# A DTW-aligned cross-attention and routed experts block on one core: context loaded as two halves, its other layout queued later, last squares' steps reordered

## What is computed

```python
def align_one(small, large):              # small: context (154 x 512), large: layernorm(x) (2048 x 512)
    D = pairwise_euclidean(small, large)  # 154 x 2048 distances
    R = dtw_cost(D)                       # R[i,j] = D[i,j] + min(R[i-1,j], R[i,j-1], R[i-1,j-1])
    i_idx, j_idx, valid = backtrack(R, T_small, T_large)
    contrib = small[i_idx] * valid[:, None]
    return zeros((T_large, d)).at[j_idx].add(contrib)

x = x + tanh(g_xattn[0]) * vmap(align_one)(ctx_1024, layernorm(x))
x = x + tanh(g_ffn[0]) * ffn(layernorm(x), gate_w, expert_w)   # top 2 of 8 experts, softmax weights
```

## Time and profile before

| | us |
|---|---|
| median of 3 runs | 623.06 |
| lowest and highest | 621.59, 623.34 |
| the profiled execution | 623.45 |
| its span, first to last instruction | 621.6 |
| TensorE busy in it | 468.9 |
| VectorE busy | 286.5 |
| ScalarE busy | 241.4 |
| GpSimd busy | 237.3 |

### The profile page before, as it was taken

One profiled execution on the slowest core, in us unless ns is written; L12 is line 12 of the kernel. 1 busy time (PEld: TensorE's weight loads), 2 busy tenths in 40 slices (PEclk: granted clock), 3 DMA queues, 4 the chain that ended last, 5 costly groups with the idle time before them and its releaser, 6 DMA issues.

```text
span 621.6 us, 7820 instructions
## 1 busy us (share of the span) xinstructions
PE 468.9 (75%) x2118; PEld 276.3 (44%) x2118; DVE 286.5 (46%) x1522; ACT 241.4 (39%) x449; POOL 237.3 (38%) x228
## 2 busy tenths in 40 slices
PE   5999667567100001828999999999999999999994
PEld 5999644344100001315445544444444444444441
DVE  4878989999988885999861400000000000000000
ACT  4477685444400000484779322222222333333331
POOL 5900230000000000004432456676567667666853
PEclk9899877977555555776999999999999999999998
DMA  8962269710051004376878957787787778678875
GB/s 253 391 221 74 70 153 251 188 27 1 0 202 69 1 1 141 124 283 214 272 191 245 283 98 134 136 160 135 120 162 133 134 141 153 113 140 153 147 125 67
DMA packets 56108, 91.78 MB, mean 148 GB/s; under 512 B 19263, under 2 KB 19263, under 8 KB 55907
## 3 DMA queue, kind: packets, MB, share of 16 engines
q0 software_dynamic: 18016, 43.00, 37.5%
q1 hardware_dynamic: 33523, 39.88, 19.5%
q10 hardware_dynamic: 4528, 8.41, 4.2%
HBM read 50.05 MB, written 41.21 MB: 147 GB/s over the span
## 4 chain that ended last, share of the span: by engine, by line
PE 59%; DVE 31%; DMA 4%; issue 4%; ACT 1%; POOL 0%; SPq 0%; POOLq 0%; ACTq 0%; DVEq 0%
PE psum L1694 40%; DVE met L923 5%; PE psum L1679 5%; PE psum L1472 5%; DVE waves L836 5%; DVE tokens L926 3%; DVE tokens L861 3%; DVE shf L827 2%; PE psum L1459 2%; DVE tokens L839 2%; DVE tokens L985 2%; PE psum L1621 2%; DVE tokens L830 2%; DMA ar<-in_ctx_dram 1%; DVE waves L826 1%
## 5 line engine op out<-in xcount | busy, mean ns | idle before, releaser
L1694 PE MATMUL psum<-big,tokens 128*128 x624 | 280.6, 593 | 0.3 <-ACT tokens L1393 0.3
L1694 PEld LDWEIGHTS psum<-big,tokens 128*128 128x128 f32 x624 | 112.5, 190 | 112.9 <-issue 112.9
L637 POOL DMA_INDIRECT tokens<-x_rows,gather_ids x78 | 79.1, 1014 | 45.7 <-issue 21.3
L650 POOL DMA_INDIRECT out_dram<-work,add_ids x40 | 63.2, 1580 | 53.6 <-DMA out_dram<-work,add_ids 26.3
L650 POOL DMA_INDIRECT out_dram<-prow,add_ids x38 | 59.9, 1577 | 45.9 <-DMA out_dram<-prow,add_ids 11.9
L657 POOL DMA_DIRECT2D out_dram<-tokens x2 | 1.8, 912 | 172.3 <-DVE tokens L985 172.3
L1403 ACT ACTIVATE work<-psum,tile_shares 128x512 f32<-128x512 f32 x40 | 27.5, 686 | 99.4 <-PE psum L1694 93.5
L1403 ACT ACTIVATE prow<-psum,tile_shares 128x512 f32<-128x512 f32 x38 | 26.1, 686 | 92.1 <-PE psum L1694 92.1
L1364 ACT ACTIVATE stage<-tokens,nm 128x512 f32<-128x512 f32 x32 | 21.7, 713 | 96.8 <-DVE tokens L985 96.7
L1679 PEld LDWEIGHTS psum<-ident,tokens 128*128 128x128 f32 x312 | 39.0, 143 | 39.0 <-issue 33.7
L1590 PE MATMUL psum<-side,work 128*128 128x2 f32 x8 | 1.9, 356 | 70.9 <-DVE work L944 70.9
(11 more groups left out here) (320 smaller groups left out, 614.2 us busy)
## 6 DMA issues: line engine op xcount, KB each, us to landing
tokens<-in_x_dram SPq DMA_DIRECT2D x16, 1024.0 KB, 11.1
stage<-in_L_ffn_expert_w_dram ACTq DMA_DIRECT2D x8, 1024.0 KB, 6.2
x_rows<-stage SPq DMA_DIRECT2D x32, 256.0 KB, 2.5
out_dram<-tokens SPq DMA_DIRECT2D x6, 1024.0 KB, 8.1
tokens<-dist_rows SPq DMA_DIRECT2D x52, 64.0 KB, 2.2
dist_rows<-work SPq DMA_DIRECT2D x16, 160.0 KB, 2.0
out_dram<-tokens POOLq DMA_DIRECT2D x2, 1024.0 KB, 5.1
dist_rows<-prow SPq DMA_DIRECT2D x5, 256.0 KB, 10.4
```

What stands on the lines that cost most here:

```text
L637: pool.indirect_dma_start(out=xin[:, n % UX, :], out_offset=None, in_=x2_d[b][:, :], in_offset=bass.IndirectOffsetOnAxis(ap=gids[:, b, j:j ...
L650: pool.indirect_dma_start(out=out_d.rearrange("b t c -> (b t) c"), in_=yout(n), in_offset=None, out_offset=bass.IndirectOffsetOnAxis(ap=ai ...
L1694: ins = nc.tensor.matmul(psum[:, UP + n % UP, :], xinT[:, n % UX, c, :], expT[:, bass.ds(own, 1), c, :].rearrange("p o d -> p (o d)"), sta ...
```

## The change

The context is loaded a second time in another layout, two halves of 77 rows on 77 partitions each (`ctxh`, in the second half of `stage`), and these loads stand first on SP's queue. `ctx_centred`, `context` and `context_turned` work on the halves. The 128 + 26 layout (`am`, `ar`) is still loaded, but behind four groups of x, and only GpSimd's splitting uses it; GpSimd now waits for its loads instead of for VectorE. One constant matrix (`turn_h`) takes the place of two, and one product that of two in `context_norms`. The context's means for the gate come from `cmean`, by one more product for each of four sums in TensorE's `ctx_gate`; two ScalarE instructions of `ctx_gate_rows` go. At the end of the front, the roots of the last group stand ahead of the distances of units 10 and 11, unit 14's max is done by ScalarE and unit 15's by VectorE, and the last squares stand after wave steps 0 and 1 and after step 2, where they stood after steps 0 to 2 and after steps 3 and 4.

```diff
...
@@ -167,7 +167,9 @@
         aa = sb("ctx_norms", [P, 2, B])
-        aam, aar = aa[:, 0, :], aa[0:SR, 1, :]
+        aam = aa[:, 0, :]
+        spare = prow[:, B * T:2 * B * T].bitcast(F32)[:, 2 * GT * SG:]
+        cmean = spare[:, 0:2 * B * G].rearrange("p (h b e) -> p h b e", h=2, b=B)
         auxs = sb("aux", [P, NT])
@@ -177,7 +179,8 @@
         stage = stagef[:, :].rearrange("p (h k c) -> p h k c", h=2, k=GT)
-        ctxc = stage[:, 0, :, :]
+        ctxc = stage[0:H, 0, :, :]
+        ctxh = stage[0:H, 1, :, :]
         sq = prow[:, B * T:2 * B * T].bitcast(F32)[:, 0:2 * GT * SG].rearrange("p (r k n) -> p r k n", r=2, k=GT)
...
@@ -426,14 +430,17 @@
         def _(sp):
+            for h in range(2):
+                sp.dma_start(ctxh[:, 2 * h:2 * h + 2, :], ctx_d[:, h * H:(h + 1) * H, :].rearrange("b p c -> p b c")).then_inc(
+                    s_ch, 16)
+            for g in ORDER[:4]:
+                sp.dma_start(x[:, GT * g:GT * g + GT, :], x_v[g]).then_inc(s_x[g], 16)
             sp.dma_start(am[:, :, :], ctx_d[:, 0:SM, :].rearrange("b p c -> p b c")).then_inc(s_ctx, 16)
-            for g in ORDER[:1]:
-                sp.dma_start(x[:, GT * g:GT * g + GT, :], x_v[g]).then_inc(s_x[g], 16)
             sp.wait_ge(s_zero, 1)
             for k in range(3):
                 sp.dma_start(ar[32 * k:32 * k + SR, :, :],
                              ctx_d[:, SM:S, :].rearrange("b p c -> p b c")).then_inc(s_ctr, 16)
-            for g in ORDER[1:]:
+            for g in ORDER[4:]:
                 sp.dma_start(x[:, GT * g:GT * g + GT, :], x_v[g]).then_inc(s_x[g], 16)
...
@@ -555,9 +560,10 @@
                            allow_small_or_imprecise_dtypes=True).then_inc(s_late, 1)
-            nc.gpsimd.memset(gwT[:, :, E], 1.0 / C).then_inc(s_late, 1)
-
-            pool.wait_ge(s_cc, 2)
+            nc.gpsimd.memset(gwT[:, :, E], 0.0).then_inc(s_late, 1)
+
+            pool.wait_ge(s_ctx, 16)
+            pool.wait_ge(s_ctr, 48)
             n = 0
...
@@ -703,21 +709,17 @@
 
-            def ctx_centred(r):
-                a = am if r == 0 else ar[0:SR3, :, :]
-                n = P if r == 0 else SR3
-                if r == 0:
-                    v.wait_ge(s_ctx, 16)
-                else:
-                    v.wait_ge(s_ctr, 48)
+            def ctx_centred(h):
+                v.wait_ge(s_ch, 32)
                 for b in range(B):
-                    ins = v.bn_stats(cst[0:n, r, b, :], a[:, b, :])
+                    ins = v.bn_stats(cst[0:H, h, b, :], ctxh[:, 2 * h + b, :])
                 link(ins)
                 for b in range(B):
-                    ins = v.bn_aggr(cmv[0:n, r, b, :], cst[0:n, r, b, :])
+                    ins = v.bn_aggr(cmv[0:H, h, b, :], cst[0:H, h, b, :])
                 link(ins)
                 for b in range(B):
-                    ins = v.tensor_scalar(ctxc[0:n, 2 * r + b, :], a[:, b, :], cmv[0:n, r, b, 0:1], None, ALU.subtract)
+                    ins = v.tensor_scalar(ctxc[:, 2 * h + b, :], ctxh[:, 2 * h + b, :], cmv[0:H, h, b, 0:1], None,
+                                          ALU.subtract)
                 ins.then_inc(s_cc, 1)
@@ -725,6 +727,7 @@
                 v.tensor_scalar(aa[:, :, :], aa[:, :, :], float(C), float(C), ALU.mult, ALU.add).then_inc(s_aam, 1)
+                v.tensor_scalar(cmean[:, :, :, E], cmv[:, :, :, 0], -2.0, None, ALU.mult).then_inc(s_aam, 1)
 
@@ -761,15 +764,15 @@
             def last_squares_by_row():
-                for u in (NU - 2, NU - 1):
-                    b, h, g = UNITS[u]
-                    v.wait_ge(s_d2, u + 1)
-                    v.wait_ge(s_dd, u - 1)
-                    if h:
-                        v.wait_ge(s_aab, 2)
-                    v.tensor_scalar(dsq[0:HP, u % 2, :], psum[0:HP, u % 2, :], (aab if h else aam)[0:HP, b:b + 1], 0.0,
-                                    ALU.add, ALU.max).then_inc(s_dv, 1)
-
+                u = NU - 1
+                b = UNITS[u][0]
+                v.wait_ge(s_d2, u + 1)
+                v.wait_ge(s_dd, u - 1)
+                v.wait_ge(s_aab, 2)
+                v.tensor_scalar(dsq[0:HP, u % 2, :], psum[0:HP, u % 2, :], aab[0:HP, b:b + 1], 0.0,
+                                ALU.add, ALU.max).then_inc(s_dv, 1)
+
+            v.memset(cmean[:, :, :, :], 0.0)
             link(v.memset(cmv[:, :, :, :], 0.0))
@@ -839,14 +842,13 @@
 
-            for s in range(0, 3):
+            for s in range(0, 2):
                 step(s)
             squares_by_token(NG - 1, (0, 1))
-            for s in range(3, 5):
-                step(s)
+            step(2)
             squares_by_token(NG - 1, (2, 3))
             last_squares_by_row()
-            for s in range(5, NS):
+            for s in range(3, NS):
                 step(s)
@@ -1186,14 +1188,11 @@
             def context_turned(n):
-                b, r = n % B, n // B
+                b, h = n % B, n // B
                 act.wait_ge(s_aTp, n + 1)
-                lo, cnt = (0, SM) if r == 0 else (SM, SR)
-                got = psum[:, AT[n], 0:CH * cnt].rearrange("p (c i) -> p c i", c=CH)
-                if r == 0:
-                    nc.scalar.mul(aT[:, b, :, 0:H], got[:, :, 0:H], -2.0)
-                nc.scalar.mul(aT[:, b, :, S + H - lo - cnt:S + H - max(lo, H)][:, :, ::-1],
-                              got[:, :, max(lo, H) - lo:cnt], -2.0).then_inc(s_aT, 1)
+                got = psum[:, AT[n], 0:CH * H].rearrange("p (c i) -> p c i", c=CH)
+                rows = aT[:, b, :, h * H:(h + 1) * H]
+                nc.scalar.mul(rows[:, :, ::-1] if h else rows, got, -2.0).then_inc(s_aT, 1)
 
@@ -1220,17 +1219,17 @@
                 b, h, g = UNITS[u]
-                if u < NU - 2:
+                if u < NU - 1:
                     act.wait_ge(s_d2, u + 1)
...
                         act.wait_ge(s_dd, u - 1)
-                    nc.scalar.activation(dsq[0:HP, u % 2, :], psum[0:HP, 6 + u % 2, :], ACT.Relu,
+                    nc.scalar.activation(dsq[0:HP, u % 2, :], psum[0:HP, u % 2 if u == NU - 2 else 6 + u % 2, :], ACT.Relu,
                                          bias=(aab if h else aam)[0:HP, b:b + 1]).then_inc(s_dq, 1)
                     act.wait_ge(s_dq, u + 1)
                 else:
-                    act.wait_ge(s_dv, u + 3 - NU)
+                    act.wait_ge(s_dv, 1)
                 if u >= 2:
@@ -1255,13 +1254,14 @@
                 roots(i - 1)
+                if i == NG - 1:
+                    roots(i)
                 if i == 2:
...
                     distances(2 * (i - 2) + h)
-            roots(NG - 1)
             def codes_laid(k):
@@ -1293,10 +1293,8 @@
                 for to, n, at in ((cgx, P, 320), (cgr, SR3, 352)):
-                    nc.scalar.mul(to[:, :, 0:E], psum[0:n, 3, at:at + B * G].rearrange("p (b e) -> p b e", e=G)[:, :, 0:E],
+                    nc.scalar.mul(to[:, :, :].rearrange("p b e -> p (b e)"), psum[0:n, 3, at:at + B * G],
                                   -0.5).then_inc(s_cgc, 1)
-                for r, (to, n) in enumerate(((cgx, P), (cgr, SR3))):
-                    nc.scalar.mul(to[:, :, E], cmv[0:n, r, :, 0], tgates[0:n, 0:1]).then_inc(s_cgc, 1)
 
@@ -1424,22 +1422,19 @@
             def context(n):
-                b, r = n % B, n // B
-                pe.wait_ge(s_cc, r + 1)
+                pe.wait_ge(s_cc, n // B + 1)
                 if n == B:
                     pe.wait_ge(s_gwc, B + 1)
-                cnt = SM if r == 0 else SR
                 for c in range(CH):
-                    ins = nc.tensor.transpose(psum[:, AT[n], c * cnt:(c + 1) * cnt], ctxc[0:cnt, n, c * P:(c + 1) * P],
-                                              ident[0:cnt, 0:cnt])
+                    ins = nc.tensor.transpose(psum[:, AT[n], c * H:(c + 1) * H], ctxc[:, n, c * P:(c + 1) * P],
+                                              ident[0:H, 0:H])
                 ins.then_inc(s_aTp, 1)
...
                 pe.wait_ge(s_aT, 2 * B)
-                nc.tensor.matmul(psum[0:HP, 7, P:P + B], turnm[:, :], aam, start=True, stop=False)
-                nc.tensor.matmul(psum[0:HP, 7, P:P + B], turnr[0:SR, :], aar, start=False, stop=True).then_inc(s_aab, 1)
+                nc.tensor.matmul(psum[0:HP, 7, P:P + B], turn_h[0:H, :], aa[0:H, 1, :], start=True, stop=True).then_inc(s_aab, 1)
 
@@ -1548,8 +1543,10 @@
                             rows = aT[:, b, c, 0:H] if h == 0 else aT[:, b, c, H:S][:, ::-1]
-                            ins = nc.tensor.matmul(psum[0:G, 3, b * S + h * H:b * S + (h + 1) * H], gwT[:, c, :], rows,
-                                                   start=(c == 0), stop=(c == CH - 1))
+                            nc.tensor.matmul(psum[0:G, 3, b * S + h * H:b * S + (h + 1) * H], gwT[:, c, :], rows,
+                                             start=(c == 0), stop=False)
+                        ins = nc.tensor.matmul(psum[0:G, 3, b * S + h * H:b * S + (h + 1) * H], cmean[0:H, h, b, :],
```

(25 more changed lines are left out.)

## The result

The changed kernel takes 627.25 us (median of 4 runs, 625.33 to 628.77), the kernel before beside it 622.95. The ratio is 1.0071, 95% interval 1.0044 to 1.0098. The profiled execution took 625.33 with a span of 623.5; it is the quickest of its four, so its trace accounts for 1.9 us of a difference of 4.3 between the medians. The forecast was 621.7, in a range from 618.8 to 624.6.

The account below looks back on a forecast made before the run. The kernel was taken as one relay: TensorE's groups of x, VectorE's wave, TensorE's expert tiles. Front 0 and tail -1.4 took the profiled 623.45 to 622.0; with the median 0.4 below, the forecast was 621.7, range 618.8 to 624.6.

Parts of the forecast that it names:

- What bounds the kernel: Whole kernel: one relay, TensorE through eight groups of x, VectorE with the wave, then TensorE with the expert tiles.
- Front, part one: Start to group 0's products: halves in at about 4.9, first products near 15.9 instead of 17.5, 1.6 us won.
- The term of 1.6 to 2.5: Front's gain taken alone: 1.6 us from earlier first products plus 0 to 0.9 us from the clock.
- Front, part two: First store of distances lands at 40.7, group 4's products start as before; front worth 0 us, at most 1.
- the slack: Ahead of group 4's products: the first store may land 2.6 us later, at 40.7, before TensorE is later.
- My bad end: First store lands only at 41.5, as the last of all early traffic: minus 0.8 us for the front.
- The skill's rule on how many engines a DMA uses: Loads of the halves: 77 partitions use 11 engines; by that rule store and forecast would be 0.75 us later.
- Tail: End of the front to wave step 8: last squares 1.3 us earlier, gain 1.4 in all, 0.6 to 1.5.
- Small parts: Added gate matmuls, later GpSimd splitting, moved loads: priced at nothing; GpSimd's idle time covers a delay of 6.
- the early traffic got quicker: Low DMA rate from 4 to 9 us goes, store lands at 38.4, front keeps 2.3: 619.4; chance 0.26.
- The tail gave what it should: Answers the case that the next chunk's load is held by something else, 0.6 or less remains: 622.7; chance 0.10.
- The rival with the clock: Ahead of group 4: store later than 40.5 and clock falls to 1.2 GHz, +1.0 us: 624.1; chance 0.14.

Follow-up runs that it names:

- tail_weights: Kernel before with the change's three tail edits and the early expert weights issued at group 5 instead of group 2; 621.69 beside 623.57, ratio 0.9976.
- 80 partitions: Changed kernel with the context's halves loaded as four loads, three of 80 partitions and one of 77; one run, 625.19 beside 623.83.
- the tail alone: Kernel before with only the change's three edits at the end of the front; 621.59 beside 623.12, ratio 0.9978.
- the front alone: Changed kernel with its three edits at the end of the front undone; 628.73 beside 624.05, ratio 1.0077.
- the 64 + 13 partitions: Changed kernel with each half of the context loaded as 64 and 13 partitions instead of 77; one run, 628.46 beside 624.05.

## Why the prediction was wrong, point by point

**What bounds the kernel**: right. A shift of group 4 and of step 8 passed through to the end unchanged but for 0.5 us.

**Front, part one**: group 0 at 10.80 is as forecast (10.9). (The byte count there mixes KB of 1000 and of 1024 bytes; that is worth less than 0.1 us.) The halves came 1.5 us later than the count by bytes said, and the first products start at 17.32, not at 15.9. Here the clock was left at the wrong place: I expected its low stretch to stay or vanish, but it moved onto group 0's transposes, 3.68 us instead of 2. What looks like 1.5 us won by group 1 (25.07 to 23.61) is mostly this, as `tail_weights` shows. The term of 1.6 to 2.5 was some 1 us at best: group 1's products start at 23.62 there, and between 22.48 and 23.61 in the nine kernels with the halves on 77 partitions.

**Front, part two**: the step that failed. The mechanism was right to the instruction: the square root of unit 2, waiting for the store of unit 0, with what stands behind it. The sequence behind it was right too: 44.32 to the end of the first squares at 49.6 is 5.3 us, as from 38.20 before. The store's landing was mis-sized: 40.7 forecast, 44.3 measured. Two terms were missing. The dip at 19 to 23 us is 1.9 us; I priced the second loading by bytes at full rate. The slow end of the queue is the other: from 41 to 44 us 3 x 149 = 0.45 MB took 3 us instead of 1.1. Together 3.7, and 40.7 + 3.7 = 44.4.

The rates up to the store's landing bear this out, before and then after:

```profile
0.00:38.10 38.10, 31.11 (x227) 30.39 (x228) 24.74 (x100) 17.94 (x42) 23.60 (x46) 0.96 0.95 332
```

```profile
0.00:38.10 38.10, 32.84 (x237) 32.37 (x238) 25.61 (x105) 17.97 (x40) 21.39 (x42) 0.91 0.94 316
38.10:44.30 6.20, 4.60 (x35) 4.32 (x33) 0.81 (x5) 0.00 (x0) 2.28 (x3) 1.00 0.71 261
```

The bytes were right: 12.65 MB before, 12.04 + 1.62 = 13.66 after, so 1.0 MB more, and I had counted 0.63 + 0.4. The rates were not: at 38.1 us the changed kernel was 0.6 MB behind (1.6 us), and from there to the landing 261 GB/s instead of 392 cost 2.1 us.

My bad end, "only where the second load of weights lands now", took that moment as fixed, while the same traffic pushed it from 41.5 to 43.1. The 3.6 us by which the store missed the slack all went into group 4; 0.3 of clock came on top (the transposes of 3.48 us).

For the dip the Trainium skill has a price that I had not weighed: "SBUF — State Buffer", the section on the DMA port swizzle, says that a transfer into partitions 0 to 31 reaches 8 of 16 ports, up to 218 GB/s. The stretch's 209 lies near that, but it is the sum of all that moved there, loads of 128 partitions among it, so it bears the rule out only in part. The length of the dip doesn't follow: 312 KB at 209 instead of 392 lose 0.7 us, and 1.9 were lost.

**The skill's rule on how many engines a DMA uses** ("DMA: Bandwidth & Descriptors"): the halves were later than by bytes, as it would have it, but with 80 partitions later still, so nothing here bears it out.

**Tail**: right. Forecast 1.4, measured 1.5 by the medians of the tail alone; the last squares' rows follow the last products by 0.7 us, and the idle time at step 8 is 1.06, forecast "near 1".

**Small parts**: right for the change as made; GpSimd's splitting ran from 24.2 to about 40.5 in its idle time. It held only for the delay of 6 that I priced; with 30 it costs VectorE 7 us.

**Rivals**: the early traffic got quicker only behind the stretch that I had priced. From 4 to 9 us it moved 195 GB/s against 211, with no 26-row load near it. From 9 to 11.5 us, before and then after:

```profile
9.00:11.50 2.50, 1.03 (x9) 1.03 (x10) 0.00 (x0) 0.34 (x1) 2.36 (x17) 1.00 1.03 275
```

```profile
9.00:11.50 2.50, 1.82 (x11) 1.59 (x12) 2.40 (x8) 0.86 (x2) 2.44 (x5) 0.50 1.04 400
```

The other two kernels that load the 26-row copies first have 283 and 263 there. So the kernel before had a dip of its own, worth 0.7 us, and the change moved it to 19 us, where it cost 1.9. The gain went into the slower start: by 12 us both kernels had moved 2.6 MB.

The tail gave what it should. The rival with the clock had the sign and the place: store later than 40.5, clock at 0.50 from 46.6 to 50. But its main term is the store, 3.6 us, and not the clock, 0.3.

**Chances**: the forecast had the store land exactly at the end of the slack, and every cost left unpriced could only make it later. With slack 0 and 1 us lost per us of delay, 0.06 for slower was far too little. This reasoning set the chances wrong; the price of a dip could have been read from the kernel before, in the stretch from 9 to 11.5 us.

**Open**: 2.4 us of the difference of the medians. Two things scatter. In the traces of the five kernels with all this traffic the store lands between 43.7 and 45.6. And behind step 8 twelve of the fourteen traces take 540.8 to 541.7 us, but that of the front alone takes 545.0 and that of the 64 + 13 partitions 543.7. Both have a stretch at the 1.2 GHz level among the expert tiles, right after TensorE waited for a gather, where the other twelve have the granted clock at 1.00. Here is the front alone, then the changed kernel:

```profile
353.04 0.66 PE L1678 MATMUL psum<-ident,tokens 128*128 128x128 f32 x4 [2.81 <-DMA tokens<-x_rows,gather_ids]
353.53 5.29 PE L1693 MATMUL psum<-big,tokens 128*128 x8
```

```profile
349.64 0.66 PE L1677 MATMUL psum<-ident,tokens 128*128 128x128 f32 x4 [1.31 <-DMA tokens<-x_rows,gather_ids]
350.13 3.60 PE L1692 MATMUL psum<-big,tokens 128*128 x8
```

The wait and the slower products make 1.5 + 1.7 = 3.2 of its 3.5 us; the edits touch nothing there. Whether the changed kernel's three other executions are longer by this or by the store can't be told from one trace of it.

## What to carry to other kernels

When a change adds bytes or loads on few partitions to a busy queue, find the first store whose buffer is waited for, and give the slack to it before the change rather than after: another pair of buffers, or loads that nobody needs yet put behind it. Price a load by the rate that loads of its own shape show in the kernel before, not by the full one. Where a landing is forecast right at the end of its slack, the unknowns all point to one side, and so must the chances. And work moved to another engine's idle time must be checked against what the neighbour does in that time.

## What was not expected of the hardware

Loads of 26 partitions beside full ones bring down what all 16 DMA engines move together, to 209 GB/s at a busy share of 1.08 from 19 to 23 us, and for longer than their bytes would take. At the head of the queue, in the kernel before, the same three came with 275.

Small VectorE instructions wait for a GpSimd instruction that runs beside them: a cast of 128x64 took 1.45 us instead of 0.16, an instruction with two tensors of 128x1 in SBUF 0.80 instead of 0.22, one of 128x65 to bf16 2.12 instead of 0.25, while scalings and a cast of 128x1 beside them stayed at 0.15. The Trainium skill ("SBUF — State Buffer", who interferes with whom) describes this as a port pair shared by VectorE and GpSimd and held for a whole instruction, with casts, some scalings and instructions of two SBUF inputs among those that need it. The rows agree.

The 1.2 GHz stretch of the start moves by several us from one kernel to the next, also where nothing ahead of it was changed: 16.0 to 19.3 before, group 0's transposes in `tail_weights`. A gain of 1 us read off one trace of this front can be only that.
